# A quantised layer whose weights are rounded earlier, by ScalarE, and whose remainders are made by TensorE

## The chip, the cores and the metric
One core of a Trainium2 chip runs the whole program. The metric is the device time of one execution in microseconds (us). The kernel before takes 1255.05 us (median of 3 runs, 1253.74 to 1255.72). Names used below: PE is TensorE, DVE is VectorE, ACT is ScalarE, POOL is GpSimd, SP is SyncE.

## The reference, cut to what matters
Six layers follow one another on x of shape (4, 16, 16, 192), that is 1,024 tokens of 192 channels: a selective scan, a neighbourhood attention, the quantised layer, a mixture of experts, a full attention, a second mixture of experts. The change concerns the third. In it (12 heads of 16 channels, 4 images of 256 tokens, `fq` rounds to int8 steps of a scale):

```python
x_norm = fq(layernorm(x, g1, beta1), s_n1)          # x is itself a layer-normed t
qkv = fq(einsum(x_norm, fq(w_qkv, s_wqkv)) + b_qkv, s_qkv)
attn = fq(einsum(q, k) * ATTN_SCALE, s_attn)
# integer softmax, on x_int = attn/s - max:
q = floor(x_int / x0_int);  r = x_int - x0_int * q;  z = r + b_int
exp_int = floor((z * z + c_int) * 2 ** (EXP_N - q))
factor = floor(2**32 / sum(exp_int));  out = floor(exp_int * factor / 2**25) / 2**7
x_attn = fq(einsum(einsum(out, v), fq(w_proj)) + b_proj, s_sv);  x = fq(x + x_attn, s_r1)
h = fq(gelu(einsum(fq(layernorm(x)), fq(w_fc1)) + b_fc1));  h = fq(einsum(h, fq(w_fc2)) + b_fc2)
x = fq(x + h, s_r2)
```

## The kernel before, in words
The program is a series of blocks. In a block each engine has its own list of instructions, executed in the order written; semaphores tie the lists together. The layer is `quantised_layer` (line 1014 on).

**Head.** SP loads the scales, seven rows of 192 numbers spread over all partitions, the biases and five weight matrices (lines 1090 and 1092). DVE normalises X into U (lines 165 to 175), makes some 20 constants of one column each (1154 to 1176), scales the seven rows (1179), normalises U into N, multiplies and shifts it by rows and rounds it (1190, 1191, 1140, 1141). Meanwhile POOL rounds the two large weights w1 and w2 (1102 to 1104), and later the projection weight. DVE rounds wqk and wv (1197 to 1199). PE transposes N (1396), makes 12 projections of 128x512 (1408) and 8 of values (1413). ACT evacuates the 12 (1330) and DVE clips and rounds each with two instructions (1140, 1141), then the values. Rounding adds and subtracts the constant MAGIC = 1.5 * 2^23 in float32. POOL copies the operands of four heads at a time to fixed places (1113), and the scores begin (1432).

**Loop.** The function `slots(b, first, second)` of each engine writes the work on images: `first` is the softmax of image b up to its sums, `second` the probabilities and the output of image b-1. The order is image 0 first only, then a loop of three with both, then second only. A slot is one head, and the stages of a head lie in successive slots. With both, an engine's slot n holds, in this order:

- PE: scores of head n into a PSUM bank (1432); four transposes of head n-2's probabilities (1440); four small matmuls of head n-3's output (1449).
- ACT: `shift` of head n+1, which reads the scores and writes lt (1336); two instructions for head n's probabilities pv (1352); the square of head n-1 (1357); the quotient of head n (1362); the copy of head n-1's transposed probabilities (1367).
- DVE: clip of lt (1218), rounding of the quotient of head n-1 (1224), maximum (1227), remainder of head n-1 (1231), the difference x_int of head n (1237), rounding of head n-1's probabilities (1243), and the product and sum for head n-2 (1252).
- POOL: the power of two as an int16 pattern (1121).

The sums of all heads end in a factor on DVE (1258 to 1263), for which ACT waits ahead of the next image.

**After the loop** the output is transposed (1461), projected (1467), requantised, normalised again, and goes through the two feed-forward products (1478, 1486).

**The scan layer** comes first. Its second block has 48 steps. In each, ACT makes one exponential of 128x1020 (line 550) into one of two PSUM pairs, DVE two products and a scan of 128x1024 (465, 472), POOL one product (435), PE the spreads and sums (600, 615). SP prefetches d_sp four steps ahead (419).

Of the kernel before, what the change touches and what calls it, by code (L numbers as in the profile page):

```python
# [14 lines left out]
BF16 = mybir.dt.bfloat16  # L15
# [9 lines left out]
NB = 4  # L25
# [166 lines left out]
KD = 4  # L192
# [6 lines left out]
NSP = 4  # L199


def scan_layer(nc, const, X, D):
# [3 lines left out]
    with ExitStack() as stack:  # L206
# [24 lines left out]
        loaded_g, loaded_w, loaded_p, loaded_s = S("loaded_g"), S("loaded_w"), S("loaded_p"), S("loaded_s")  # L231
        cleared, zeroed, proj, padded, tapped, convd, activated, gated = (
# [43 lines left out]
        with nc.Block() as block:  # L276
            @block.sync
            def _(sp_):
# [107 lines left out]
        ex = ctx.sb("ex", [DI, 2, T])  # L386
# [17 lines left out]
        tile = lambda a, t: a[:, t * P:(t + 1) * P]  # L404
        with nc.Block() as block:
            @block.sync
            def _(sync):
# [18 lines left out]
                for n in range(NSP, N):  # L426
                    spread(n)
# [83 lines left out]
            def _(act):  # L511
# [23 lines left out]
                for i in range(1, KD):  # L535
                    for j in range(2):
                        take(i, j)
                act.wait_ge(A_done, 2)
                for n in range(N):
# [4 lines left out]
                    if n % NG < 2:  # L544
# [462 lines left out]
EXP_N = 30  # L1007
(S_N1, S_WQKV, S_QKV, S_ATTN, S_WPROJ, S_SV, S_R1, S_N2, S_WFC1, S_ACT, S_WFC2, S_M2, S_R2) = range(13)

(K_QKV, K_ATTN, K_X0, K_BI, K_CI, K_INV, K_QB, K_CLAMP, K_NX0, K_PROJ, K_FC1, K_FC2, K_T0, K_T1, K_MAGIC, K_FLOOR) = range(16)  # L1010


def quantised_layer(nc, K, X, D, ln):

    with ExitStack() as stack:
        ctx = Ctx(nc, stack)
        U = ctx.sb("q_U", [P, NT, C])  # L1020
        N = ctx.sb("q_N", [P, NT, C])
        Ni = ctx.sb("q_Ni", [P, NT, C], BF16)
        nT = ctx.sb("q_nT", [CH, 2, T], BF16)
        sc = ctx.sb("q_sc", [P, 13])
        rc = ctx.sb("q_rc", [P, 13])
        kf = ctx.sb("q_kf", [P, 16])
        rows = ctx.sb("q_rows", [P, 7, C])
        bqk = ctx.sb("q_bqk", [P, 6])
        b1 = ctx.sb("q_b1", [P, FT])
        wqk_f = ctx.sb("q_wqk_f", [CH, 2 * 6 * P])  # L1030
        wqk = ctx.sb("q_wqk", [CH, 2 * 6 * P], BF16)
        wv_f = ctx.sb("q_wv_f", [CH, 2 * C])
# [24 lines left out]
        pv = ctx.sb("q_pv", [P, 2, QT, L])  # L1057
        pi = ctx.sb("q_pi", [P, 2, QT, L], BF16)
# [8 lines left out]
        loaded, w_loaded, vec, w_quantised, quantised, first_ln = (  # L1067
            S("loaded"), S("w_loaded"), S("vec"), S("w_quantised"), S("quantised"), S("first_ln"))
        scaled, constants, normed, turned_n, n_sb = S("scaled"), S("constants"), S("normed"), S("turned_n"), S("n_sb")
        proj, evac, qk_ready, v_proj, v_ready = S("proj"), S("evac"), S("qk_ready"), S("v_proj"), S("v_ready")  # L1070
        taken, pool_past = S("taken"), S("pool_past")
        scores, shifted, clipped, negmax, diff, quot, whole, rest, expo, square, expd, factor = (
            S("scores"), S("shifted"), S("clipped"), S("negmax"), S("diff"), S("quot"), S("whole"), S("rest"),
            S("expo"), S("square"), S("expd"), S("factor"))
        prob, floored, turned, turned_sb, summed, o_sb = (
            S("prob"), S("floored"), S("turned"), S("turned_sb"), S("summed"), S("o_sb"))
        o_turned, oT_sb, o_proj = S("o_turned"), S("oT_sb"), S("o_proj")
        act_past = S("act_past")
        h_steps = S("h_steps")
# [4 lines left out]
        SLOTS = NH + 2  # L1084

        with nc.Block() as block:
            @block.sync
            def _(sync):
                for dst, src in ((sc, "q_scales"), (rows, "q_rows"), (bqk, "q_bqk"), (b1, "q_b1")):
                    sync.dma_start(dst[:], D[src].partition_broadcast(P) if src in ("q_scales", "q_rows") else D[src]).then_inc(loaded, 16)  # L1090
                for dst, src in ((wqk_f, "q_wqk"), (wv_f, "q_wv"), (wp_f, "q_wp"), (w1_f, "q_w1"), (w2_f, "q_w2")):
                    sync.dma_start(dst[:], D[src]).then_inc(w_loaded, 16)

            @block.gpsimd
            def _(pool):
                step = Chain(pool, w_quantised)
                pool.wait_ge(scaled, 1)
                pool.wait_ge(w_loaded, 80)

                def quantise(f, i, r):  # L1100
                    n = f.shape[0]
                    step(pool.tensor_scalar(f[:], f[:], rc[0:n, r:r + 1], 127.0, ALU.mult, ALU.min))
                    step(pool.tensor_scalar(f[:], f[:], -128.0, MAGIC, ALU.max, ALU.add))
                    step(pool.tensor_scalar(i[:], f[:], -MAGIC, None, ALU.add))

                quantise(w1_f, w1, S_WFC1)
                quantise(w2_f, w2, S_WFC2)

# [6 lines left out]
                def powers(b, more):  # L1115

                    for h in range(NH):
                        pool.wait_ge(whole, b * NH + h + 1)
# [3 lines left out]
                                           float((127 + EXP_N) * 128), ALU.mult, ALU.add).then_inc(expo, 1)  # L1122
# [13 lines left out]
            def _(v):  # L1136
                step = Chain(v, vec)

                def clip_round(dst, src, signal):
                    step(v.tensor_scalar(src, src, 127.0, -128.0, ALU.min, ALU.max))  # L1140
                    return v.tensor_scalar(dst, src, MAGIC, -MAGIC, ALU.add, ALU.add).then_inc(signal, 1)
# [20 lines left out]
                step(v.tensor_tensor(k(K_QKV), k(K_QKV), r(S_QKV), ALU.mult))  # L1162
                step(v.tensor_scalar(k(K_ATTN), k(K_ATTN), r(S_ATTN), HE ** -0.5, ALU.mult, ALU.mult))
# [9 lines left out]
                step(v.tensor_scalar(k(K_QB), k(K_INV), -0.5, -0.5, ALU.mult, ALU.add))  # L1173
                step(v.tensor_scalar(k(K_CLAMP), k(K_X0), float(EXP_N), None, ALU.mult))
                step(v.tensor_scalar(k(K_NX0), k(K_X0), -1.0, None, ALU.mult))

                step(v.tensor_scalar(bqk[:], bqk[:], r(S_QKV), None, ALU.mult))
                for row, unit in ((0, S_N1), (1, S_N1), (2, S_N2), (3, S_N2), (4, S_QKV), (5, S_SV), (6, S_M2)):
                    step(v.tensor_scalar(rows[:, row, :], rows[:, row, :], r(unit), None, ALU.mult))
                v.memset(kf[:, K_T0:K_T1 + 1], 0.0).then_inc(constants, 1)  # L1180

                def row(i):
                    return rows[:, i, :].unsqueeze(1).broadcast_to([P, NT, C])

                def normed_ints(use, g, beta):

                    v.wait_ge(ln.out, NT * use)
                    ln.vector(v, use, U, N, 1e-6)
                    v.wait_ge(ln.out, NT * (use + 1))
                    step(v.tensor_tensor(N[:], N[:], row(g), ALU.mult))  # L1190
                    step(v.tensor_tensor(N[:], N[:], row(beta), ALU.add))
# [1269 lines left out]
```

## Time and profile before
| | |
|---|---|
| median of the runs shown | 1255.05 us |
| the profiled execution | 1259.88 us, span 1257.9 us |
| busy: PE, DVE, ACT, POOL | 66%, 73%, 48%, 29% of the span |
| granted TensorE clock, mean | 0.795 of full speed |

The profile is of one execution. An interval of idle time is put down to what released the engine. Times of instructions are from their start to the end of their writes, so two instructions of an engine in a row can overlap a little: "spacing" below is from one start to the next. TensorE's clock has two levels, 1.2 GHz (0.50 of full speed) and 2.4 GHz (1.00).

### The profile page before, as it was taken

Reading aid. Unit: us, or ns where it says so; the run is one execution under the profiler, and the core shown is the slowest. Engines: PE = TensorE matmul, PEld = TensorE weight load, DVE = VectorE, ACT = ScalarE, POOL = GpSimd, SP = SyncE. Lnnn points to the kernel's source line nnn. Section 1 sums busy time; section 2 is a strip of 40 time slices with the busy share of each in tenths; the row PEclk is TensorE's granted clock in tenths of the full one; section 3 lists DMA queues with packets and bytes.
Section 4 is the critical chain, followed back from the end, with each engine's and each line's share of the span. In section 5 each row is a group of like instructions: output and inputs, shape, how many; then the busy total and the mean of one; then the engine's idle time right before and its main releaser. Section 6 shows DMA issues by size and latency. Waiting matters only on the chain. (4 is left out here: it accounts for less than half of the span.)

```text
span 1257.9 us, 16849 instructions
## 1 busy us (share of the span) xinstructions
PE 825.4 (66%) x5554; PEld 576.7 (46%) x5554; DVE 921.5 (73%) x1731; ACT 598.2 (48%) x938; POOL 362.2 (29%) x309
## 2 busy tenths in 40 slices
PE   6799999859894041122224336599999747449990
PEld 2333333335783020011114225599888725339990
DVE  5679999936655989999993777488888533628871
ACT  3743333215331046789897223277766122328870
POOL 0036666430000822222210002532222510054444
PEclk8789999969997565555555676899999959659995
DMA  8075565130003000000000008299995110628932
GB/s 258 13 205 151 150 151 150 34 75 1 1 1 88 0 1 1 0 1 0 0 0 1 0 1 224 77 232 267 263 266 160 39 44 1 170 83 258 272 115 81
DMA packets 65821, 120.59 MB, mean 96 GB/s; under 512 B 11152, under 2 KB 40784, under 8 KB 65744
## 3 DMA queue, kind: packets, MB, share of 16 engines
q1 hardware_dynamic: 62672, 113.31, 33.4%
q0 software_dynamic: 3072, 6.30, 1.7%
q8 instruction: 43, 0.70, 0.2%
q14 instruction: 34, 0.28, 0.1%
HBM read 102.08 MB, written 17.50 MB: 95 GB/s over the span
## 5 line engine op out<-in xcount | busy, mean ns | idle before, releaser
L435 POOL TENSOR_TENSOR hC<-hs,Cb 128x1024 f32<-128x1024 f32 x47 | 110.7, 2355 | 129.3 <-DVE hs L472 129.3
L1726 POOL CAST m_h_hi<-m_h 128x512 f16<-128x512 f32 x62 | 54.0, 871 | 247.4 <-DVE m_h L1801 247.4
L472 DVE TENSOR_TENSOR_SCAN hs<-ps_l,dBu 128x1024 f32<-128x1024 f32 x48 | 110.0, 2291 | 2.8 <-ACT ps_l L550 1.2
L1440 PE MATMUL ps_l<-identb,q_pi 128*128 128x128 bf16 x192 | 29.2, 307 | 112.3 <-DVE q_pi L1243 112.3
L550 ACT ACTIVATE ps_l<-d_sp,Am 128x1020 f32<-128x1020 f32 x48 | 53.5, 1115 | 89.9 <-DVE hs L472 89.7
L615 PE MATMUL ps_l<-hC,selT 128*96 128x512 f32 x192 | 93.3, 609 | 1.5 <-POOL hC L435 1.5
L600 PE MATMUL ps_l<-du,sel 96*128 96x512 f32 x192 | 90.5, 593 | 1.4 <-DVE dBu L465 1.4
L1809 DVE TENSOR_TENSOR m_h_lo<-m_h,m_h_hi 128x512 f16<-128x512 f32 x62 | 42.8, 691 | 46.5 <-POOL m_h_hi L1726 41.9
L1121 POOL TENSOR_SCALAR q_e<-q_qi 128x512 int16<-128x512 bf16 x48 | 31.3, 652 | 153.7 <-DVE q_qi L1224 153.7
L1440 PEld LDWEIGHTS ps_l<-identb,q_pi 128*128 128x128 bf16 x192 | 16.5, 130 | 128.4 <-DVE q_pi L1243 128.4
L2092 PE MATMUL ps_m<-m_wd_hi,m_h_hi 128*128 128x192 f16 x248 | 62.9, 254 | 8.4 <-DVE m_h_lo L1809 4.8
L1999 ACT ACTIVATE m_act<-ps_m 128x512 f32<-128x512 f32 x62 | 36.8, 594 | 66.0 <-PE ps_m L2074 55.8
L465 DVE TENSOR_TENSOR dBu<-ps_l,Bb 128x512 f32<-128x512 f32 x96 | 60.7, 673 | 4.9 <-PE ps_l L600 4.8
L2094 PE MATMUL ps_m<-m_wd_hi,m_h_lo 128*128 128x192 f16 x248 | 63.0, 254 | 0.0
L2093 PE MATMUL ps_m<-m_wd_lo,m_h_hi 128*128 128x192 f16 x248 | 63.0, 254 | 0.0
L1432 PE MATMUL ps_l<-q_qkb 16*128 16x256 bf16 x96 | 27.2, 402 | 52.4 <-ACT q_lt L1336 44.4
L1726 POOL CAST g_h_hi<-g_act 128x512 f16<-128x512 f32 x45 | 43.7, 988 | 60.6 <-ACT g_act L2003 60.6
L600 PEld LDWEIGHTS ps_l<-du,sel 96*128 96x128 f32 x192 | 34.2, 188 | 51.2 <-DVE dBu L465 37.2
L615 PEld LDWEIGHTS ps_l<-hC,selT 128*96 128x96 f32 x192 | 27.4, 162 | 58.8 <-POOL hC L435 31.9
L1352 ACT ACTIVATE q_pv<-q_ex,q_kf,q_fac 128x256 f32<-128x256 f32 x96 | 51.8, 591 | 0.5 <-DVE q_fac L1263 0.5
L2070 PE MATMUL ps_m<-m_xt,m_wa_hi 128*128 128x256 f16 x184 | 50.3, 273 | 0.8
L2071 PE MATMUL ps_m<-m_xt,m_wa_hi 128*128 128x256 f16 x184 | 50.2, 273 | 0.0
(484 smaller groups left out, 2807.2 us busy)
## 6 DMA issues: line engine op xcount, KB each, us to landing
d_sp<-scan_d SPq DMA_DIRECT2D x48, 512.0 KB, 4.5
m_sta<-in_m_ua SPq DMA_DIRECT2D x25, 512.0 KB, 4.9
m_stb<-in_m_ub SPq DMA_DIRECT2D x50, 256.0 KB, 6.3
m_std<-in_m_dn SPq DMA_DIRECT2D x25, 384.0 KB, 8.2
g_std<-in_g_dn SPq DMA_DIRECT2D x15, 576.0 KB, 5.9
g_sta<-in_g_ua SPq DMA_DIRECT2D x15, 384.0 KB, 3.5
g_stb<-in_g_ub SPq DMA_DIRECT2D x30, 192.0 KB, 4.7
scratch_x<-zero SPq DMA_DIRECT2D x1, 4416.0 KB, 20.0
```

Of the source, the lines that this page charges most:

```text
L435: pool.tensor_tensor(hC[:, n % 2, :], hs[:, n % 2, :], Cb[:, which(n), :], ALU.mult).then_inc(weighted, 1)
L465: v.tensor_tensor(dBu[:, n % 2, half * BANK:(half + 1) * BANK], ps[:, 4 + half, :], Bb[:, which(n), half * BANK:(half + 1) * BANK], ALU.mu ...
L472: v.tensor_tensor_scan(hs[:, n % 2, ::step], dA(n)[:, ::step], dBu[:, n % 2, ::step], 0.0, ALU.mult, ALU.add).then_inc(scanned, 1)
L550: act.activation(dst[:, :, o:o + L - 1], d_sp[:, n % NSP, :].rearrange("p (b t) -> p b t", t=L)[:, :, o:o + L - 1], ACT.Exp, scale=Am[:, c ...
L600: pe.matmul(ps[:, 4 + half, :], sel[:, n % NG, :], du[:, n // NG, half * BANK:(half + 1) * BANK], start=True, stop=True).then_inc(du_bc, 1)
L615: mm = pe.matmul(ps[0:DI, 6 + half, :], selT[:, n % NG, :], hC[:, n % 2, half * BANK:(half + 1) * BANK], start=(n == STEPS), stop=(m == ST ...
L1352: act.activation(pv[:, h % 2, q, :], ex[:, h, q, :], ACT.Identity, scale=fac[:, h, q:q + 1], bias=kf[:, K_FLOOR:K_FLOOR + 1]).then_inc(pro ...
L1726: pool.tensor_copy(h_hi[:, b % 2, q, :], src).then_inc(h_high, 1)
L2070: pe.matmul(out, wa_hi[a][:, col], x[:, 0, :], start=True, stop=False)
L2092: pe.matmul(out, h_hi[:, b % 2, f // 2, tok], wd_hi[a][:, col], start=(f == 0), stop=False)
L2093: pe.matmul(out, h_hi[:, b % 2, f // 2, tok], wd_lo[a][:, col], start=False, stop=False)
L2094: mm = pe.matmul(out, h_lo[:, b % 2, f // 2, tok], wd_hi[a][:, col], start=False, stop=(f == tiles - 1))
```

## The change
- **Weights.** Scales, inverse scales and the five rounded weight matrices live for the whole program (`K["q"]`). SP loads each float weight into the buffer `ex` of the scan layer, free by then, at scan steps 5, 13, 21, 29 and 37, and ACT rounds it there with four instructions (Identity, Relu, Relu, Identity), one after the exponential of each of four steps. The quantised layer has neither the loads nor the rounding on POOL and DVE.
- **Folded norm.** The two norms ahead of the projections become one: statistics of X once, the second variance worked out from the first, N written once; gain and offset are given in ACT's evacuation of the transposed N as its scale and bias. U is written later, behind image 0. Scaled rows: one ahead of image 0, four behind it.
- **Rounding at ACT's writes.** lt, xi, qi, pi, the operands and the values are fp16 numbers centred at 1536, so that the write itself rounds; DVE's roundings of the quotient (1224) and of the probabilities (1243) are gone, clips stay.
- **Remainders by PE.** Two matmuls of 128x128 by 128x512 fp16 (identity times xi, and -x0 times identity times qi) make the remainder in PSUM bank 5 or 6; ACT squares it in place; DVE's remainder (1231) is gone. DVE takes over the copy of the transposed probabilities, with the centre subtracted.
- **Projections split.** Six projections (images 0 and 1) stand ahead of the loop, six and the values inside the slots of image 0.

The slots after the change, to the order of the instructions:

```diff
 @block.vector, slot n
-  clip lt(h) ; qi = qv + MAGIC - MAGIC (g) ; max(h) ; ri(g) = qi * -x0 + xi ; xi(h) x2
-  pi(g) = pv + MAGIC - MAGIC ; ex(n-2) x2
+  clip lt(h) ; max(h) ; xi(h) x2     # waits rest(h-2)
+  v.wait_ge(turned, pb * NH + g + 1)
+  PT(g) <- ps[2 + g % 2] as F16, - CENTRE
+  ex(n-2) x2                         # from ps[5 + e % 2]
+  if first and not second and 1 <= n < 7: operand(5 + n)
+  if first and not second and 7 <= n < 11: values(n - 7)
 @block.scalar, slot n
   shift(b, h + 1)
-  pv(h) x2 ; square(g) ri -> zz ; quot(h) xi -> qv ; PT(g) <- ps
+  pi(h) x2 (F16) ; square(g) in place in ps[5 + g % 2]   # waits rest(g)
+  quot(h) xi -> qi (F16)
+  if first and not second and n < 6: evacuate(6 + n)
 @block.tensor, slot n
-  h, g, e = n, n - 2, n - 3
+  h, r, g, e = n, n - 1, n - 1, n - 2
   scores(h)
   transposes(g)                      # waits prob(g) instead of floored(g)
+  if first and 0 <= r < NH:
+      pe.wait_ge(quot, b * NH + r + 1)
+      pe.wait_ge(expd, (b * NH + max(r - 1, 0)) * QT)
+      pe.matmul(ps[:, 5 + r % 2, :], K["identh"], xi[:, r % 2], start=True, stop=False)
+      pe.matmul(ps[:, 5 + r % 2, :], XI[:, :], qi[:, r % 2, :], start=False, stop=True).then_inc(rest, 1)
   output(e)
+  if first and not second and n < 6: project(6 + n)
+  if first and not second and 6 <= n < 10: project_values(n - 6)
```

In the scan layer:

```diff
 @block.sync
   for n in range(NSP, N):
+      w = (n - Q_FIRST) // Q_EACH        # Q_FIRST = 5, Q_EACH = 8
+      if (n - Q_FIRST) % Q_EACH == 0 and w < len(q_weights):
+          sync.wait_ge(soft_vec, 3 * KD) if w == 0 else sync.wait_ge(qw["quantised"], 4 * w)
+          sync.dma_start(staged(w)[:, :], D[q_weights[w][0]]).then_inc(q_loaded, 16)
       spread(n)
 @block.scalar
   exponential of step n
+      w, i = divmod(n - Q_FIRST, Q_EACH)
+      if w >= 0 and i < 4 and w < len(q_weights):
+          integer(w, i)    # i = 0 waits q_loaded; then Identity, Relu, Relu, Identity
```

## Rows read from the trace of the kernel before

**Rows 1.** Busy time by engine in two stretches, the layer's head and its loop:
```profile
396.00:466.00 70.00, 12.37 (x60) 6.31 (x60) 63.50 (x129) 12.45 (x17) 31.76 (x14) 0.56 0.14 40
...
514.00:560.00 46.00, 13.04 (x104) 7.69 (x104) 44.44 (x122) 42.55 (x70) 9.09 (x15) 0.50 0.00 1
```
**Rows 2.** Instructions in order of time, head; start, duration, engine, line:
```profile
396.86 2.18 DVE L165 BATCH_NORM_STATS2 ln_st<-X 128x6 f32<-128x192 f32 x8 [2.40 <-PEq L56]
...
398.16 0.43 SPq L1090 DMA_DIRECT2D q_b<-in_q_b  x1
...
403.16 0.93 DVE L1161 TENSOR_TENSOR q_kf<-q_sc 128x1 f32<-128x1 f32 x5
...
408.46 24.23 DVE L1179 TENSOR_SCALAR q_rows<-q_rows,q_rc 128x192 f32<-128x192 f32 x7
...
432.66 3.14 POOL L1104 TENSOR_SCALAR q_w<-q_w_f 128x1152 bf16<-128x1152 f32 x1
...
448.39 8.57 PE L1408 MATMUL ps_l<-q_nT,q_wqk 96*128 96x512 bf16 x24 [2.08 <-DVE q_wv L1199]
...
460.43 2.11 POOL L1113 COPY q_qkb<-q_qk 128x256 bf16<-128x256 bf16 x6 [24.64 <-DVE q_qk L1141]
...
465.46 0.61 PE L1432 MATMUL ps_l<-q_qkb 16*128 16x256 bf16 x4 [7.18 <-DVE q_vi L1141]
```
**Rows 3.** In order of time, loop with both stages, one head:
```profile
546.96 0.41 DVE L1243 TENSOR_SCALAR q_pi<-q_pv 128x512 bf16<-128x512 f32 x1
...
547.42 0.60 PE L1440 MATMUL ps_l<-identb,q_pi 128*128 128x128 bf16 x4 [2.81 <-DVE q_pi L1243]
...
547.82 0.30 PE L1449 MATMUL ps_l<-q_vi,q_PT 128*128 x4
...
548.05 0.60 PE L1432 MATMUL ps_l<-q_qkb 16*128 16x256 bf16 x2
...
548.69 0.78 ACT L1336 ACTIVATE q_lt<-ps_l,q_kf 128x512 f32<-128x512 f32 x1
...
549.37 0.91 DVE L1231 SCALAR_TENSOR_TENSOR q_ri<-q_qi,q_kf,q_xi 128x512 bf16<-128x512 bf16 x1
549.37 1.08 ACT L1352 ACTIVATE q_pv<-q_ex,q_kf,q_fac 128x256 f32<-128x256 f32 x2
...
550.35 0.71 ACT L1357 ACTIVATE q_zz<-q_ri,q_kf 128x512 f32<-128x512 bf16 x1
550.85 0.41 DVE L1243 TENSOR_SCALAR q_pi<-q_pv 128x512 bf16<-128x512 f32 x1
550.97 0.81 ACT L1362 ACTIVATE q_qv<-q_xi,q_kf 128x512 f32<-128x512 bf16 x1
```
**Rows 4.** Issues of transfers at the layer's start; KB each, us from issue to landing:
```profile
q_b<-in_q_b SPq DMA_DIRECT2D x1, 3.0 KB, 3.5
```
**Rows 5.** DVE's groups by shape, whole span; busy, mean ns of one, idle before:
```profile
L1224 DVE TENSOR_SCALAR q_qi<-q_qv 128x512 bf16<-128x512 f32 x48 | 19.9, 415 | 3.4 <-ACT q_qv L1362 3.4
...
L741 DVE CAST n_Q<-ps_l 96x512 f16<-96x512 f32 x12 | 8.2, 682 | 1.1 <-PE ps_l L890 1.1
...
L1141 DVE TENSOR_SCALAR q_Ni<-q_N 128x1536 bf16<-128x1536 f32 x2 | 1.9, 960 | 0.1
...
L1780 DVE COPY m_xd<-ps_m 128x768 f16<-128x768 f16 x2 | 1.1, 558 | 1.2 <-PE ps_m L2021 1.2
```
**Rows 6.** In order of time, first instruction of each image, of the drain, and behind it:
```profile
513.93 1.45 ACT L1336 ACTIVATE q_lt<-ps_l,q_kf 128x512 f32<-128x512 f32 x2 [3.08 <-DVE q_fac L1263]
...
565.22 1.45 ACT L1336 ACTIVATE q_lt<-ps_l,q_kf 128x512 f32<-128x512 f32 x2 [0.97 <-DVE q_fac L1263]
...
666.53 2.07 ACT L1352 ACTIVATE q_pv<-q_ex,q_kf,q_fac 128x256 f32<-128x256 f32 x4 [0.54 <-DVE q_fac L1263]
...
686.27 3.65 PE L1461 MATMUL ps_l<-ident,q_Os 128*96 128x128 f32 x16 [0.67 <-ACT q_Os L1372]
```
**Rows 7.** In order of time, one step of the scan layer on ACT:
```profile
82.32 1.11 ACT L550 ACTIVATE ps_l<-d_sp,Am 128x1020 f32<-128x1020 f32 x1 [2.39 <-DVE hs L472]
```

More of the change, by code:

```diff
@@ L199 @@
 NSP = 4
+Q_FIRST = 5
+Q_EACH = 8
 def scan_layer(nc, const, X, D):
@@ L298, in _ @@
                 pool.memset(const["all"][:, :], 1.0).then_inc(constants, 1)
+                for n, value in enumerate((MAGIC, 128.0 - MAGIC, 255.0, 127.0)):
+                    pool.memset(qw["steps"][:, n:n + 1], value).then_inc(constants, 1)
             @block.vector
@@ L1084, in quantised_layer @@
         SLOTS = NH + 2
+        LATE = (2, 3, 4, 7)
+        order = [(half, o) for half in range(NHALF) for o in range(6)]
+        home = lambda n: n % 4 if n < 6 else LATE[n % 4]
         with nc.Block() as block:
@@ L1088, in _ @@
             def _(sync):
[L1089 to L1092, printed above, removed]
+                for dst, src in ((cols, "q_cols"), (rows, "q_rows"), (bqk, "q_bqk"), (b1, "q_b1")):
+                    sync.dma_start(dst[:], D[src].partition_broadcast(P) if src == "q_rows" else D[src]).then_inc(loaded, 16)
             @block.gpsimd
             def _(pool):
[L1096 to L1107, printed above, removed]
                 def take(b, group):
@@ L1162, in _, with integers @@
                 step(v.tensor_tensor(k(K_QKV), k(K_QKV), r(S_QKV), ALU.mult))
+                v.tensor_scalar(bqk[:], bqk[:], r(S_QKV), CENTRE, ALU.mult, ALU.add).then_inc(scaled, 1)
+                def integers(dst, part, src, steps, at, signal):
+                    v.tensor_scalar(part, src, -CENTRE, 127.0, ALU.add, ALU.min).then_inc(steps, 1)
+                    v.wait_ge(steps, at)
+                    v.tensor_scalar(dst, part, -128.0, None, ALU.max).then_inc(signal, 1)
+                for n in range(2 * NHALF):
+                    half, c = divmod(n, 2)
+                    at = slice(half * BANK, (half + 1) * BANK)
+                    v.wait_ge(centred, n + 1)
+                    integers(nT[:, c, at], nh[:, c, at], nh[:, c, at], n_part, n + 1, n_ready)
                 step(v.tensor_scalar(k(K_ATTN), k(K_ATTN), r(S_ATTN), HE ** -0.5, ALU.mult, ALU.mult))
@@ L1172, in _ @@
                 step(v.reciprocal(k(K_INV), k(K_X0)))
-                step(v.tensor_scalar(k(K_QB), k(K_INV), -0.5, -0.5, ALU.mult, ALU.add))
+                step(v.tensor_scalar(k(K_QB), k(K_INV), -0.5, CENTRE - 0.5, ALU.mult, ALU.add))
                 step(v.tensor_scalar(k(K_CLAMP), k(K_X0), float(EXP_N), None, ALU.mult))
[L1175 to L1191, printed above, removed]
-                    clip_round(Ni[:], N[:], normed)
@@ L1201, in _, with operand @@
+                step(v.tensor_scalar(k(K_SQUARE), k(K_XC), CENTRE, k(K_BI), ALU.mult, ALU.add))
+                v.tensor_scalar(XI[:, :], K["ident"][:, :], k(K_XC), -1.0, ALU.mult, ALU.mult).then_inc(constants, 1)
+                def operand(n):
+                    half, o = order[n]
                     v.wait_ge(evac, n + 1)
-                    clip_round(qk[:, n * BANK:(n + 1) * BANK], qf[:, n % 4, :], qk_ready)
-                for n in range(NT // 2):
+                    at = o * T + half * BANK
+                    integers(qk[:, at:at + BANK], qh[:, n % 4, :], qh[:, n % 4, :], q_part, n + 1, qk_ready)
@@ L1211, in slots @@
+                for n in range(6):
+                    operand(n)
                 def slots(b, first, second):
@@ L1271, in _, with clip_round, row @@
                 v.wait_ge(factor, NB)
+                def clip_round(dst, src, signal):
+                    step(v.tensor_scalar(src, src, 127.0, -128.0, ALU.min, ALU.max))
+                    return v.tensor_scalar(dst, src, MAGIC, -MAGIC, ALU.add, ALU.add).then_inc(signal, 1)
+                def row(i):
+                    return rows[:, i, :].unsqueeze(1).broadcast_to([P, NT, C])
                 def requantised(src, unit, add_to, out_unit):
@@ L1421, in slots @@
+                for n in range(6):
+                    project(n)
+                pe.wait_ge(constants, 1)
                 def slots(b, first, second):
@@ L1451, in slots @@
                             mm.then_inc(summed, 1)
+                        if first and not second and n < 6:
+                            project(6 + n)
+                        if first and not second and 6 <= n < 10:
+                            project_values(n - 6)
                 slots(0, True, False)
+                pe.wait_ge(v_ready, 4)
                 with pe.Fori(1, NB) as b:
```

341 lines of the change are left out of this document (195 added, 146 removed).

## The prediction
> **What bounds the kernel now.** I read two windows first. In the layer's head DVE is busy 63.5 of 70 us while PE is busy 12.4; in the loop DVE is busy 44.4 of 46 us, ACT 42.6 counted with overlaps, PE 13.0, and the granted clock is 0.50, the lower level, throughout [rows 1]. So DVE sets both. Then the timeline. The head runs from the first statistics at 396.86 to the first scores at 465.46, 68.6 us. The reader is to see one odd row: seven scalings of a 192-column row take 24.23 us, 3.46 each, and they end when POOL comes to the last of its roundings of w1 and w2 (432.66) [rows 2]. In the loop one DVE instruction comes back every 3.89 us (546.96 to 550.85): that is the price of a head, DVE's instructions back to back [rows 3]. An image is 51.3 us (513.93 to 565.22), the first 48.5 (465.43 to 513.93), three with both stages 152.6 (513.93 to 666.53), the drain 19.7 (to 686.27) [rows 2, 6].
>
> **The head.** Gone are POOL's rounding and with it the 24 us, the second statistics, gain, offset, rounding of N and of wqk, wv on DVE, and six of twelve projections plus the values. I count what is left from 396.86 as time 0.
> Statistics of X (2.2) and 0.7 more, as now. The column operations wait for the last of four loads: issued at 398.16 and 3.5 to land, so 4.8 [rows 2, 4]. Two column operations, four of the second variance, a square root on ACT and back, two more: nine small instructions of 0.19 (five in 0.93 [rows 2]) and two handovers, to 6.9. Eight writes of N at 0.30 each (five such stretches of 192 columns by the 0.53 ns a column below, plus overhead) end at 9.3. PE transposes them as it arrives, 16 at 0.23 (3.65 for 16 [rows 6]), to 10.9; ACT's four evacuations of 0.78 with 0.68 spacing [rows 3] end near 12.2. DVE has nine more constants (10.9), then two clips for each of four pieces.
> A clip of fp16 into fp16 or bf16 is not in this trace. From above: the same with a float32 side, 0.415 for 512 columns; with 0.960 for 1,536 that is 0.53 ns a column and 0.14 fixed [rows 5]. From below: the fixed part. Nearest on 16-bit data: out of PSUM, float32 512 columns cost 0.682, fp16 768 columns 0.558, so a column costs half [rows 5]. I halve the column here too: 0.28 for 512, spacing 0.20; a clip pair is 0.52 (0.79 by the upper row).
> Two pieces are done at 12.0, all at 13.0. 21 constants at 0.19 follow on DVE, to 17.1; PE's first projections (0.86 for two matmuls at the lower clock) and ACT's first four evacuations lie beside them. Six operands at 0.52: 20.2. POOL's first two copies, 0.35 each (2.11 for six [rows 2]): scores at 21.0. I add 0.5 for gaps: 21.5, and -47.1 us. With the upper price it is 24.2.
> The Trainium skill (VectorE: DVE Perf Modes, "What auto-detection actually checks") lets a one-source instruction with 16-bit data on both sides in SBUF take four elements a cycle where float32 takes two; that is the halved column, and the trace has no row for it. Were the page wrong, its absence would cost the 2.7 us named.
>
> **The loop: sums.** A head on DVE loses the rounding of the quotient, that of the probabilities and the remainder (0.34 + 0.34 + 0.83 in spacing) and gains the copy of PT (0.34), which ACT loses: from 3.89 to about 2.5 [rows 3, 5]. ACT has `shift` 0.68, two pi 0.98, square 0.58 to 0.62, quotient 0.81: 3.05 [rows 3]. By sums a head would be ACT's 3.0. PE gains two matmuls of 512 columns, 0.43 each (24 took 8.57, part at the upper clock; 0.43 is 512 columns at 1.2 GHz) [rows 2].
>
> **The loop: order.** The sum is not what ends last. PE's list says: scores(n+1), transposes(n), rest(n), output(n-1), then scores(n+2). rest(n) waits for quot(n), which is the last instruction of ACT's slot n; and ACT's slot n+1 begins with shift(n+2), which waits for scores(n+2). In between ACT can do nothing, its list is in order: pi(n+1), square(n) and quot(n+1) stand behind shift(n+2). So one head is a ring:
> - shift to quotient's end on ACT: 0.68 + 0.98 + 0.58 + 0.81 = 3.05 (548.69, 549.37, 550.35, 550.97 and its 0.81; the copy of PT that sits between two heads is gone) [rows 3];
> - handover 0.05 (547.37 to 547.42), two rest matmuls 0.86, output 0.23 (547.82 to 548.05), scores 0.60, handover 0.04 (548.65 to 548.69): 1.80 [rows 3].
> Together 4.85 us a head against 3.89. DVE and POOL lie inside it: clip, maximum and difference need 2 us after a shift and have nearly a whole head.
> Before, the same place held a softer ring: transposes, output, scores, 1.27 us, with ACT's copy of PT beside them [rows 3].
> What the fp16 clips cost does not matter here: DVE has 2 us to spare in either case.
>
> An image with both stages, from its first shift: shift(2) at 5.0 (quotient of head 0 at 2.5 to 3.3, rest, scores), shift(11) nine rings later at 48.6, quot(10) to 51.7, square(10) behind rest(10), quot(11) to 54.2, rest 1.1, square 0.7, DVE's two products 0.95, factor and handover 1.6: 58.6. Three: 175.7 against 152.6, +23.1.
>
> Image 0: no pi (0.98 less) but a projection of 0.86 behind rest in PE slots 0 to 5 and two tiles of values (0.64) in 6 to 9. ACT's part of a ring is 2.07, PE's 2.41, then 2.19, then 1.55. shift(2) is at 6.3, four rings of 4.48, four of 4.26, one of 3.62: shift(11) at 44.9; the same end: 53.8. ACT's evacuations and DVE's operands fit inside. Then DVE writes four scaled rows and U (12 instructions, about 4.6) ahead of its first clip, of which 3.6 are late for the next image. 57.4 against 48.5: +8.9.
>
> **The drain** has on ACT only pi, 12 x 0.98, and 2.3 behind it (transposes, copy, output, Os): 14.0 against 19.7, -5.7 [rows 3, 6].
>
> **Scan layer.** A rounding of 1,536 columns is below 1.5 x 1.11 = 1.67, against 2.39 that ACT idles in a step [rows 7]; 20 of them, hidden, 0. A load is issued some four steps ahead of its use, a step being 3.5. If the cover were gone: up to 20 x 1.6.
>
> **Sum.** -47.1 + 8.9 + 23.1 - 5.7 = -20.8. Behind the loop nothing changes. The profiled run was 1259.88 and the median is 1255.05; the change is taken off both alike: 1234.3 as a median.
>
> **Rivals.**
> 1. *The clock rises in the loop.* PE would be busy about half of a head (0.61 for transposes, 1.71 in one run) where it is busy 28% now at 0.50; the head's 12 us of work did lift the mean there to 0.56 [rows 1]. At 2.4 GHz rest, output and scores take about 1.0, a ring 4.1: 0.74 less for 30 rings and 1.1 less for ten, -33 if always, -17 if half the time: 1218. Against it: each rise shortens PE's share and so undoes itself. The Trainium skill (TensorE: Matmul & The Clock Gate, "Part 1: The HAM clock gate") says that the default is throttled and activity releases it, which speaks for this case; it names no case such as scores on 16 rows. Chance 0.2.
> 2. *ACT's sum sets the pace*, PE running ahead of the ring: 3.05 a head. 1.80 less for 30 rings and 1.8 less for ten: 1234 - 72 = 1162. It needs scores(n+2) not to stand behind rest(n), and in the order of the diff they do. Chance 0.07.
> 3. *Slower: the roundings in the scan steps are not hidden.* If a step with one grows by its whole 1.6 and the first of each matrix waits for its load too (five waits of 2), +42: 1276. It decides from +21 us on, about 1.0 for each of the 20 steps. For it: the steps' scan on DVE waits on ACT's exponential; against it: the 2.39 idle in each step. Chance 0.08.
> 4. *The stall of 24 us has another cause than POOL's roundings* and stays with the scaled rows: five rows instead of seven, +17, and 1251. Against it: the same instruction's first cases in the row and its end with POOL's work. Chance 0.03.
>
> **Chances.** The forecast holds 0.62, its own range 1222 to 1247 from the head's clip prices (3), gaps in the ring (0.2 for 40 rings, 8) and some rise of the clock in image 0 (-5). Faster by over 0.2% (2.5 us, about what a measurement of this kernel can tell): 0.88; within 0.2%: 0.03; slower 0.09. The range takes in half of rival 1: 1208 to 1249.
>
> **What would show it.** First scores 21 to 24 us after the layer's first statistics. In the loop ACT's `shift` idle about 1.8 us, released by PE's scores, and PE's rest matmuls released by ACT's quotient; a head 4.8 to 4.9 us; DVE busy near 55%; clock 0.50. Image 0 near 57 us, the others near 58.6, the drain near 14. Scan steps still 3.5 us. Heads of 3.0 to 4.2 us or a scan step over 3.6 would make it wrong.

## The result and the profile after

The changed kernel takes 1239.38 us (median of 4 runs, 1238.26 to 1242.96) beside 1254.67 us for the kernel before on the same chip (4 runs, 1253.74 to 1255.72): ratio 0.9883, 95% interval 0.986 to 0.9905, that is 15.3 us less, where 20.8 less was forecast. The profiled execution of the changed kernel took 1238.26 us, its span is 1236.5 us.

The head first, in order of time (start, duration, engine, line; in brackets the idle time ahead and what ended it). It answers to [rows 2]:
```profile
391.45 2.18 DVE L1169 BATCH_NORM_STATS2 q_st<-X 128x6 f32<-128x192 f32 x8 [2.49 <-PEq L56]
...
396.12 0.22 DVE L1176 TENSOR_SCALAR q_cols<-q_cols,q_rc 96x2 f32<-96x2 f32 x1 [1.75 <-DMA q_b<-in_q_b]
...
398.03 2.41 DVE L1187 TENSOR_SCALAR q_N<-X,q_mv,q_rs 128x192 f32<-128x192 f32 x8
...
403.21 2.88 PE L1457 MATMUL ps_l<-q_nT,q_wqk 96*128 96x512 bf16 x12 [1.34 <-DVE q_nT L1201]
...
408.33 0.29 DVE L1199 TENSOR_SCALAR q_qh<-q_qh 128x512 f16<-128x512 f16 x1
...
411.79 2.11 POOL L1132 COPY q_qkb<-q_qk 128x256 bf16<-128x256 bf16 x6 [144.22 <-DVE q_qk L1201]
...
412.67 0.58 PE L1486 MATMUL ps_l<-q_qkb 16*128 16x256 bf16 x2 [6.58 <-POOL q_qkb L1132]
```
From the first statistics to the first scores it is 21.2 us, where it was 68.6: the row of 24.23 us is gone, and so are the second statistics and the roundings.

One head of the loop with both stages, in order of time, beside [rows 3]:
```profile
484.43 0.61 PE L1500 MATMUL ps_l<-q_xi,identh 128*128 128x512 f16 x1 [0.75 <-ACT q_qi L1407]
...
484.83 0.63 PE L1501 MATMUL ps_l<-q_qi,q_XI 128*128 128x512 f16 x1
...
485.25 0.30 PE L1508 MATMUL ps_l<-q_vi,q_PT 128*128 x4
...
485.49 0.60 PE L1486 MATMUL ps_l<-q_qkb 16*128 16x256 bf16 x2
486.13 0.78 ACT L1381 ACTIVATE q_lt<-ps_l,q_kf 128x512 f16<-128x512 f32 x1 [1.83 <-PE ps_l L1486]
486.81 1.08 ACT L1397 ACTIVATE q_pi<-q_ex,q_kf,q_fac 128x256 f16<-128x256 f32 x2
486.94 0.29 DVE L1253 TENSOR_SCALAR q_lt<-q_lt 128x512 f16<-128x512 f16 x1 [1.99 <-ACT q_lt L1381]
...
487.79 0.64 ACT L1401 ACTIVATE ps_l<-ps_l,q_kf 128x512 f32<-128x512 f32 x1
...
488.36 0.81 ACT L1407 ACTIVATE q_qi<-q_xi,q_kf 128x512 f16<-128x512 f16 x1
...
489.30 0.60 PE L1500 MATMUL ps_l<-q_xi,identh 128*128 128x512 f16 x1 [0.75 <-ACT q_qi L1407]
```
Read it as a ring: TensorE's remainder waits for ScalarE's quotient, output and scores stand behind the remainder, ScalarE's `shift` waits 1.83 us for the scores, and the next quotient stands behind `shift`. The remainder comes back after 4.87 us (484.43 to 489.30), where a head cost 3.89 before. VectorE, which had hardly a gap before, is idle 1.99 us ahead of its clip.

The first instruction of each image, and of the drain, on ScalarE, and the first behind the drain on TensorE (beside [rows 6]):
```profile
467.59 1.45 ACT L1381 ACTIVATE q_lt<-ps_l,q_kf 128x512 f16<-128x512 f32 x2 [2.54 <-DVE q_fac L1288]
...
473.92 0.81 ACT L1407 ACTIVATE q_qi<-q_xi,q_kf 128x512 f16<-128x512 f16 x1 [3.91 <-DVE q_xi L1260]
...
530.31 1.45 ACT L1381 ACTIVATE q_lt<-ps_l,q_kf 128x512 f16<-128x512 f32 x2 [2.22 <-DVE q_fac L1288]
...
589.20 1.45 ACT L1381 ACTIVATE q_lt<-ps_l,q_kf 128x512 f16<-128x512 f32 x2 [2.22 <-DVE q_fac L1288]
...
647.93 11.90 ACT L1397 ACTIVATE q_pi<-q_ex,q_kf,q_fac 128x256 f16<-128x256 f32 x24 [2.06 <-DVE q_fac L1288]
...
661.96 3.65 PE L1525 MATMUL ps_l<-ident,q_Os 128*96 128x128 f32 x16 [0.67 <-ACT q_Os L1414]
```
Image 0 takes 54.9 us from the first scores, the three images 62.7, 58.9 and 58.7, the drain 14.0. The 62.7 holds a wait of 3.91 us for VectorE, which writes the scaled rows and U first.

Busy time by engine in the head and in image 1 (columns as in [rows 1]):
```profile
391.00:413.00 22.00, 6.61 (x30) 4.12 (x30) 16.74 (x84) 8.81 (x13) 1.21 (x4) 0.66 0.08 23
...
468.00:530.00 62.00, 26.54 (x144) 11.01 (x144) 38.62 (x124) 36.62 (x61) 9.49 (x18) 0.50 0.00 1
```
In the loop no engine is near full: VectorE 62%, ScalarE 59%, TensorE 43%, at a granted clock of 0.50. With no engine near full and one short wait coming back in every head, a ring is the thing to suspect; the experiments test it.

The scan layer, by groups (busy us, mean ns of one, idle ahead):
```profile
L587 ACT ACTIVATE ps_l<-d_sp,Am 128x1020 f32<-128x1020 f32 x48 | 53.5, 1115 | 71.5 <-DVE hs L495 71.3
...
L571 ACT ACTIVATE ex<-ex,q_steps,q_rc 96x1536 f32<-96x1536 f32 x2 | 3.3, 1652 | 0.0
```
ScalarE's idle time ahead of the exponentials has shrunk from 89.9 to 71.5 us, and the 48 steps take 164.7 us as before (76.49 to 241.2, and 72.41 to 237.1): the 20 roundings went into idle time. Those of 1,536 columns, the longest, took 1.56 us, or 1.65 with a scale as in the row.

### The profile page after: what moved, and what is told of

Its sections match the earlier page's. It is cut to its first block and busy times, and to the rows that moved or that the text cites. A ratio compares the mean times of both kernels' runs of the same rounds, so it can differ in the third digit from the quotient of the medians.

```text
span 1236.5 us, 16872 instructions
## 1 busy us (share of the span) xinstructions
PE 868.6 (70%) x5650; PEld 585.1 (47%) x5650; DVE 830.0 (67%) x1627; ACT 590.7 (48%) x912; POOL 327.1 (26%) x304
## 5 line engine op out<-in xcount | busy, mean ns | idle before, releaser
L587 ACT ACTIVATE ps_l<-d_sp,Am 128x1020 f32<-128x1020 f32 x48 | 53.5, 1115 | 71.5 <-DVE hs L495 71.3
L1494 PE MATMUL ps_l<-identh,q_pi 128*128 128x128 f16 x192 | 29.1, 307 | 78.1 <-ACT q_pi L1397 78.1
L1140 POOL TENSOR_SCALAR q_e<-q_qi 128x512 int16<-128x512 f16 x48 | 30.4, 632 | 193.9 <-ACT q_qi L1407 118.4
L1381 ACT ACTIVATE q_lt<-ps_l,q_kf 128x512 f16<-128x512 f32 x48 | 37.1, 778 | 84.4 <-PE ps_l L1486 74.5
L1500 PE MATMUL ps_l<-q_xi,identh 128*128 128x512 f16 x48 | 29.1, 606 | 55.2 <-ACT q_qi L1407 55.2
L2067 ACT ACTIVATE m_act<-ps_m 128x512 f32<-128x512 f32 x62 | 36.8, 594 | 62.2 <-PE ps_m L2142 58.1
L1253 DVE TENSOR_SCALAR q_lt<-q_lt 128x512 f16<-128x512 f16 x48 | 14.1, 293 | 73.7 <-ACT q_lt L1381 73.4
L1494 PEld LDWEIGHTS ps_l<-identh,q_pi 128*128 128x128 f16 x192 | 16.5, 130 | 95.1 <-ACT q_pi L1397 95.1
L1397 ACT ACTIVATE q_pi<-q_ex,q_kf,q_fac 128x256 f16<-128x256 f32 x96 | 50.8, 589 | 2.1 <-DVE q_fac L1288 2.1
```

Of the source, the lines that this page charges most:

```text
L587: act.activation(dst[:, :, o:o + L - 1], d_sp[:, n % NSP, :].rearrange("p (b t) -> p b t", t=L)[:, :, o:o + L - 1], ACT.Exp, scale=Am[:, c ...
L1397: act.activation(pi[:, h % 2, q, :], ex[:, h, q, :], ACT.Identity, scale=fac[:, h, q:q + 1], bias=kf[:, K_FLOOR:K_FLOOR + 1]).then_inc(pro ...
L1494: mm = pe.transpose(ps[:, 2 + g % 2, 0:L].bitcast(F16)[:, kt * L + q * P:kt * L + (q + 1) * P], pi[:, g % 2, q, kt * P:(kt + 1) * P], K["i ...
```

## The experiments

Theory: the loop is bound by the ring of one quotient, one remainder, one scores, one `shift`, because TensorE's list puts the next scores behind a remainder that waits for ScalarE's last instruction. Main rival: the new work has its price in any order.

**Scores one head ahead.** The changed kernel, but for one thing:
```diff
-                        if first and h < NH:
+                        for h in ((0, 1) if n == 0 else (n + 1,)):
+                            if not first or h >= NH: continue
                             ... scores(h)
```


> The changed kernel, with PE's scores one head earlier in its list: scores(n+1), transposes(n-1), rest(n-1), output(n-2). Ring theory (quotient on ACT, rest, output and scores on PE, then shift on ACT, 4.87 us a head in the profile after): the ring is cut, ACT's own sum of 3.05 us a head is next, DVE's 2.8 just under it; 30 heads with both stages and 10 of image 0 lose 1.5 to 1.8 each, so 1239 - 64 = 1175 us (1165 to 1190), and ACT's wait for scores ahead of its shift goes from 1.83 to under 0.2 us. Rival A (the loop is slow because PE at the lower clock is short of time, or because each fp16 write or PSUM read is slower than counted, not because of the order): within 10 us of 1239. Rival B (DVE's chain of clip, maximum and difference inside one slot is next at once): a head of 3.8 to 4.0 us, about 1205.

Measured: 1168.23 us (1167.93 to 1171.44), ratio 0.929 (0.9257 to 0.9324). In order of time, one head:
```profile
474.00 0.82 ACT L1407 ACTIVATE q_qi<-q_xi,q_kf 128x512 f16<-128x512 f16 x1
...
474.71 0.78 ACT L1381 ACTIVATE q_lt<-ps_l,q_kf 128x512 f16<-128x512 f32 x1
...
474.95 0.60 PE L1502 MATMUL ps_l<-q_xi,identh 128*128 128x512 f16 x1 [0.72 <-ACT q_qi L1407]
...
475.37 1.10 ACT L1397 ACTIVATE q_pi<-q_ex,q_kf,q_fac 128x256 f16<-128x256 f32 x2
...
476.35 0.65 ACT L1401 ACTIVATE ps_l<-ps_l,q_kf 128x512 f32<-128x512 f32 x1
...
476.92 0.82 ACT L1407 ACTIVATE q_qi<-q_xi,q_kf 128x512 f16<-128x512 f16 x1
```
and the loop's busy time:
```profile
460.00:590.00 130.00, 82.80 (x486) 37.22 (x485) 110.01 (x357) 115.17 (x200) 26.71 (x48) 0.50 0.00 1
```
Inside an image no wait stands ahead of `shift` any more, ScalarE runs almost without a gap, and a head is its sum, 2.92 us. The same instructions in another order are 71 us faster by the medians (69.4 from the layer's start to the end of the drain in the profiles, 74 by the ratios): the theory holds. The clock is 0.50 although TensorE is busy for 64% of the time.

**A third matmul in the remainder**, in the order of the change:
```diff
-  pe.matmul(ps[5 + r % 2], identh, xi, start=True, stop=False)
+  pe.matmul(ps[5 + r % 2], identh, xi, start=True, stop=True)
+  pe.matmul(ps[5 + r % 2], identh, xi, start=True, stop=False)
```


> The changed kernel with one matmul more per head in the rest group (identity times xi written once more ahead of the two, its result overwritten), 0.43 us at the lower clock. Ring theory: every head of the 40 or so in the ring grows by the whole 0.43, +17 to +19 us over the changed kernel, 1257; a head 5.30 us. Rival A (PE has slack, since it is busy 43% of the loop): 0, 1239. Rival C (the added work lifts the clock in the loop): below 1239, heads near 4.2.

Measured: 1259.73 us (1257.24 to 1263.79), ratio 1.0014 (0.9998 to 1.003). Over the changed kernel that is 20 us by the medians and 16 by the ratios. ScalarE's `shift`, twice in a row:
```profile
501.04 0.78 ACT L1381 ACTIVATE q_lt<-ps_l,q_kf 128x512 f16<-128x512 f32 x1 [2.26 <-PE ps_l L1486]
...
506.33 0.78 ACT L1381 ACTIVATE q_lt<-ps_l,q_kf 128x512 f16<-128x512 f32 x1 [2.26 <-PE ps_l L1486]
```
A head is 5.29, 0.42 more, and the wait for scores grows by as much (1.83 to 2.26). In the profiles each of the four images is 5.1 us longer, 20.5 together: all 48 heads pay, where 40 were expected to. TensorE is far from busy and yet each of these microseconds counts: they lie on the ring.

**The same third matmul, with the scores ahead** (both diffs together).


> Scores one head ahead, and the same third matmul of 512 columns in each head's rest group that cost 17 to 20 us in the order of the change. Theory (the ring over ScalarE and TensorE was the price; with the ring cut TensorE is no longer in series with ScalarE, and has about 0.4 us of slack ahead of the square): 0 to +4 us against the kernel with the scores ahead, 1168 to 1172. Rival (the remainders on TensorE cost their own time in any order): +17 us, about 1185.

Measured: 1173.88 us (1171.42 to 1179.11), ratio 0.9341 (0.931 to 0.9372), 5.6 us over the kernel with the scores ahead, by medians of different runs. The square now waits:
```profile
496.96 0.66 ACT L1401 ACTIVATE ps_l<-ps_l,q_kf 128x512 f32<-128x512 f32 x1 [0.65 <-PE ps_l L1504]
```
In the profiles it is 4.2 us up to the end of the drain. That is a fifth to a third of the price in the ring, and a little more than the 0 to 4 expected: TensorE's slack ahead of the square was 0.37 us (475.98, the end of the second matmul, to 476.35), less than the matmul's 0.43. A head is 3.01 where it was 2.92. Each of the three images is 1.7 us longer than with the scores ahead alone (41.3 against 39.6 for the second), about half of it where one image ends and the next begins; image 0 is not longer.

**The remainder back on VectorE**, all else as changed: VectorE makes it as float32 with one scalar_tensor_tensor, ScalarE squares it from there into PSUM, TensorE's two matmuls are gone.
```diff
+  v.scalar_tensor_tensor(ri[g % 2], qi[g % 2], k(K_T0), xi[g % 2], MULT, ADD)   # K_T0 = -x0
-  pe.matmul(... identh, xi ...) ; pe.matmul(... XI, qi ...)
-  act.activation(ps[5 + g % 2], ps[5 + g % 2], Square)
+  act.activation(ps[5 + g % 2], ri[g % 2], Square)
```


> The changed kernel with the remainder given back to DVE (one scalar_tensor_tensor of 128x512, as before, between the maximum and the difference); the two rest matmuls are gone and ACT squares from SBUF into PSUM. All else of the change stays. Ring theory: PE's part of the ring is gone; DVE's sum becomes 3.3 to 3.4 us a head, ACT's 3.1: heads of 3.4 to 3.6, about 1.35 less in 30 and about 1.0 less in 10 of image 0: 1239 - 50 = 1189 us. Rival A (the remainders on PE were a relief of DVE and the loop is slow for another reason): slower than 1239, since DVE gets 0.83 us a head more: up to +40.

Measured: 1186.1 us (1183.86 to 1188.14), ratio 0.9418 (0.9384 to 0.9452). In order of time:
```profile
485.76 0.78 ACT L1389 ACTIVATE q_lt<-ps_l,q_kf 128x512 f16<-128x512 f32 x1 [0.44 <-PE ps_l L1495]
486.31 0.74 DVE L1262 SCALAR_TENSOR_TENSOR q_ri<-q_qi,q_kf,q_xi 128x512 f32<-128x512 f16 x1
...
489.00 0.78 ACT L1389 ACTIVATE q_lt<-ps_l,q_kf 128x512 f16<-128x512 f32 x1 [0.17 <-PE ps_l L1495]
```
A head is 3.0 to 3.5 us, VectorE almost without a gap. So in the order of the change the part "remainders by PE" costs 53 us by the medians (58 by the ratios) of what the rest of the change had won: it takes 0.8 us from VectorE's sum, but its two matmuls, 0.9 us, tie ScalarE's quotient to the next scores, and that closes the ring.

**The quotient on VectorE**, in the order of the change:
```diff
+  v.tensor_scalar(qi[h % 2], xi[h % 2], k(K_INV), k(K_QB), MULT, ADD)   # behind xi(h)
-  act.activation(qi[h % 2], xi[h % 2], Identity, scale=K_INV, bias=K_QB)
```


> The order of the change, the quotient of each head written by VectorE (tensor_scalar, 512 half-precision elements, about 0.3 us) in place of ScalarE's 0.81 us. Theory: the ring stays, scores - shift - ... - rest - scores, but is shorter by about 0.5 us where the quotient was on it, 4.87 to 4.3 a head: 48 x 0.5 = -24, about 1215 us (1205 to 1225). Rival (the ring runs over ScalarE's list alone, so that taking 0.81 from it frees all of that, and VectorE's 3.2 us a head are not waited for): 4.05 a head, -39, about 1200.

Measured: 1207.42 us (1206.26 to 1208.11), ratio 0.96 (0.9584 to 0.9616). In order of time:
```profile
497.45 0.78 ACT L1385 ACTIVATE q_lt<-ps_l,q_kf 128x512 f16<-128x512 f32 x1 [1.72 <-PE ps_l L1484]
498.13 1.08 ACT L1401 ACTIVATE q_pi<-q_ex,q_kf,q_fac 128x256 f16<-128x256 f32 x2
...
499.27 0.61 PE L1492 MATMUL ps_l<-identh,q_pi 128*128 128x128 f16 x4 [1.93 <-ACT q_pi L1401]
...
499.67 0.63 PE L1498 MATMUL ps_l<-q_xi,identh 128*128 128x512 f16 x1
...
500.75 0.60 PE L1484 MATMUL ps_l<-q_qkb 16*128 16x256 bf16 x2
...
501.47 0.78 ACT L1385 ACTIVATE q_lt<-ps_l,q_kf 128x512 f16<-128x512 f32 x1 [1.72 <-PE ps_l L1484]
```
The ring is still there (`shift` waits 1.72 us for the scores), but runs another way: behind the probabilities instead of the quotient, `shift`, two pi, transposes, remainder, output, scores, 4.02 us. Quotient and square both left it and the transposes, 0.40, came in; the 4.3 expected had taken out 0.5 only. The 1207 lie in the range of the theory, 8 us below its middle. The rival's number for a head was near (4.05) for a reason that the wait contradicts.

**The weights alone**: the kernel before with nothing but the scan layer's roundings and without those on POOL and VectorE. The edit on the kernel before:
```diff
 @block.scalar, scan steps
+  integer(w, i)                           # 20 instructions, as in the change
 @block.gpsimd, quantised_layer
-  quantise(w1_f, w1) ; quantise(w2_f, w2) ; quantise(wp_f, wp_f)
 @block.vector, quantised_layer
-  rounding of wqk, wv ; reciprocal of the scales
```


> The kernel before with one part of the change only: scales and the five weight matrices rounded by ACT in the scan steps; POOL's and DVE's roundings and loads in the quantised layer are gone, all else as before. Theory: the seven scaled rows cost 0.32 us each instead of 3.46 (-22.0), DVE's roundings of wqk and wv go (-4.1), the scan steps stay at 3.50 us: 1254.7 - 26 = 1228.5 us. Rival (the stall of 24 us has another cause than POOL's roundings): rows stay at 3.46, only -4: 1250. Rival (roundings in the scan steps are not hidden): steps 13 to 44 grow and part of the 26 is given back, up to 20 x 1.6: 1228 to 1260.

Measured: 1236.47 us (1234.41 to 1239.7), ratio 0.9833 (0.9797 to 0.9869): 20.6 us less. In order of time:
```profile
402.64 2.45 DVE L1191 TENSOR_SCALAR q_rows<-q_rows,q_rc 128x192 f32<-128x192 f32 x7
...
436.48 0.61 PE L1439 MATMUL ps_l<-q_qkb 16*128 16x256 bf16 x4 [7.12 <-DVE q_vi L1155]
```
The same seven scaled rows take 2.45 us where they took 24.23 [rows 2], with no rounding on POOL beside them; the head is 45.2 us (from 391.32), 23.4 less. The scan steps are as long as before (161.2 us from the second exponential to the last), so the roundings are hidden here too. The 26 us expected were too many. VectorE's roundings of wqk and wv had stood in time in which it would have waited for the projections: without them it waits 5.18 us ahead of its first clip, where it waited 1.94. The loop is 1.0 longer, and this profile has the longer of the two tails told of below.

From the layer's start to the end of the drain, in the profiles, this part alone wins 22.5 us (289.4 to 267.0) and all five together 18.9 (to 270.5). The medians, 20.6 and 15.3, point the same way, but the intervals of the ratios overlap a little.

**The kernel before, scores ahead**, the first diff on it.


> The kernel before, with TensorE issuing each head's scores one head earlier and nothing else changed. Theory (before, VectorE's instructions stood back to back at 3.89 us a head and TensorE's place in the order cost nothing; the ring was made by the change, which put the remainders between quotient and scores): 0 us, 1253 to 1259. Rival (the order of the scores held back the kernel before as well, so that the gain of the scores ahead has little to do with the change): 0.3 us or more a head, 1243 or less.

Measured: 1256.18 us beside 1258.33, ratio 0.9983 (0.9966 to 1.0). VectorE's rounding of the probabilities, twice:
```profile
546.50 0.41 DVE L1243 TENSOR_SCALAR q_pi<-q_pv 128x512 bf16<-128x512 f32 x1
...
550.40 0.41 DVE L1243 TENSOR_SCALAR q_pi<-q_pv 128x512 bf16<-128x512 f32 x1
```
3.90 us a head, as before, and 289.4 us from the layer's start to the end of the drain in both profiles. Where VectorE had hardly a gap the order on TensorE was worth nothing; the interval of the ratio leaves room for 4 us at most. The change made the ring the bound.

**Scores ahead, U and four rows late.**
```diff
-  scaled rows 0, 1, 3, 4 and U(0..7)     # ahead of image 1
   loop of images, drain
+  scaled rows 0, 1, 3, 4 and U(0..7)     # behind VectorE's last head
```


> Scores one head ahead, and VectorE's four scaled rows and eight U tiles, which stood between the second half of the first head group and the first clamp of image 1, moved behind the last head. Theory (in the kernel with the scores ahead ScalarE's own sum paces the loop; its one long wait, 3.9 us for q_xi at the start of image 1, is VectorE's 3.29 us of U and some 0.5 us of rows): the wait goes, the work lands beside the drain, where VectorE has little else; 1168 - 3.6 = about 1164.5 us (1162 to 1167). Rival (VectorE, with about 2.8 us a head, is as much the pace as ScalarE, or U is waited for behind the drain): no gain, 1167 to 1171.

Measured: 1164.52 us (1162.72 to 1171.26), ratio 0.9274 (0.924 to 0.9308). Image 1 is 39.7 us where it was 43.5 with the scores ahead alone (458.89 to 502.37), 3.8 less; the medians, of different runs, differ by 3.7.

**With the quotient on GpSimd besides:**
```diff
+  pool.tensor_scalar(qi[h % 2], xi[h % 2], kf[K_INV], kf[K_QB], MULT, ADD)
-  act.activation(qi[h % 2], xi[h % 2], Identity, scale=K_INV, bias=K_QB)
```


> Scores ahead and U late, and the quotient of each head written by GpSimd (tensor_scalar, 512 half-precision elements, one scalar pointer for each of its two steps) in place of ScalarE's 0.81 us. ScalarE's sum falls from 2.92 to 2.1 us a head, VectorE's of about 2.75 becomes the pace. Theory A (GpSimd's instructions of this size leave VectorE's alone): 2.75 to 2.8 a head, 48 x 0.15 = -7, about 1157 us (1152 to 1163). Theory B (VectorE's clips, differences and copies stretch while GpSimd works, as its scaled rows did beside the roundings of w1 and w2, 3.46 against 0.3 us): slower than 1164.5, 1170 us or more, with VectorE's instruction of 0.29 us at 0.5 or more where it lies beside GpSimd's.

Measured: 1160.42 us (1158.03 to 1163.54), ratio 0.9222 (0.9194 to 0.9249), the fastest median; its interval and the one above still overlap. From the layer's start to the end of the drain the profiles say 6.5 us less. The time is that of theory A; what theory B says of VectorE's instructions is seen too, in image 0. In order of time:
```profile
426.20 0.73 POOL L1146 TENSOR_SCALAR q_e<-q_qi 128x512 int16<-128x512 f16 x1 [0.22 <-POOL q_qi L1141]
426.37 0.71 DVE L1259 TENSOR_SCALAR q_lt<-q_lt 128x512 f16<-128x512 f16 x1
...
506.58 0.29 DVE L1259 TENSOR_SCALAR q_lt<-q_lt 128x512 f16<-128x512 f16 x1
...
506.85 0.62 POOL L1146 TENSOR_SCALAR q_e<-q_qi 128x512 int16<-128x512 f16 x1 [0.32 <-DVE q_ex L1279]
```
The last two rows are of image 2. There GpSimd's instructions fall beside VectorE's products and maximum, the clip takes 0.29, and the image takes 36.8 us (496.10 to 532.85) instead of 39.7. In image 0 the clip meets GpSimd: five of its twelve clips take 0.71, where two did with the quotient on ScalarE, and the image takes 45.7 (414.05 to 459.71) instead of 43.1. That the clips are all of these 2.5 us is not shown.

**The changed kernel once more.**


> The changed kernel once more beside the others: 1238 to 1243 us, head period 4.87 us in the last three images; the tail behind the drain, from the last ScalarE read of the scores to the next layer, again about 69.5 us if the lower granted clock of the projections belongs to the kernel, 66.9 if it was chance.

Measured: 1242.09 us (1239.01 to 1244.38) beside 1257.8, ratio 0.9885 (0.9868 to 0.9902). The projections behind the drain, first in the profile of the result, then in this one, by window:
```profile
660.00:672.00 12.00, 10.22 (x48) 9.47 (x48) 1.41 (x3) 2.87 (x5) 0.00 (x0) 0.54 0.01 1
```
```profile
662.00:674.00 12.00, 9.52 (x59) 8.59 (x56) 2.87 (x5) 2.87 (x5) 0.00 (x0) 0.80 0.00 1
```
One kernel shows both: a granted clock of 0.54, 32 projections that are busy for 7.8 us, and 69.5 us from the drain to the next layer; or 0.80, 5.5 and 66.9. Of the twelve profiles of this case five have the longer tail (69.2 to 69.7) and seven the shorter (66.8 to 67.2).

## Why the prediction was right, and where it was off

- **What bounds the kernel now:** right, as far as it was tried. In the loop VectorE had hardly a gap, and moving the scores in TensorE's list did nothing. No run shortened VectorE's list in the loop and left the rest as it was.
- **The head, -47.1:** right, 68.6 to 21.2, -47.4. The fp16 clip, priced by halving the column, was 0.28 and took 0.28 to 0.29. The stall was POOL's roundings (weights alone: 2.45 for 24.23); rival 4 falls. The 3.46 us for each scaled row is a mean of two kinds: two rows took 0.32 before POOL began, and five 4.1 to 5.4.
- **The order in the loop, 4.85 a head:** right, 4.87. The wait of `shift` is 1.83 where 1.8 was named. VectorE is busy 62%, not "near 55%"; the terms given for its head (3.89 less 1.51, plus 0.34) add up to 2.7 and not to "about 2.5". Nothing in the forecast rests on that.
- **An image with both stages, 58.6:** 58.7 to 58.9; with 3.9 us of the first taken off, three are 176.4 against 175.7.
- **Image 0, 53.8 and 3.6 late:** 54.9 and 3.9. The ring there is 4.57 against 4.48 while operands are projected, mostly because two projections hold TensorE 0.99 us (422.18 to 423.17), not 0.86; after them it is 4.36 against 4.26.
- **The drain, 14.0:** 14.0. **The scan steps, 0:** 164.7 both times; rival 3 falls (a rounding of 1,536 columns took 1.56 to 1.65, below the bound of 1.67).
- **Rival 1, the clock rises:** no, 0.50 throughout the loop, and even at the 64% of the loop with the scores ahead. The Trainium skill's account (TensorE: Matmul & The Clock Gate, "Part 1: The HAM clock gate") that activity releases the throttled clock was cited for this rival; this loop does not show it, though behind the drain the clock did rise (0.54 and 0.80 above).
- **Rival 2, ScalarE's sum sets the pace:** not in the order of the diff; in the other order exactly that, 2.92 where 3.05 was written.

The step that was off is "Behind the loop nothing changes": in the profile shown it is 69.5 us where it was 66.9, and that is TensorE's clock, which is not of the change, since the same kernel has both. In the profile up to the end of the drain the change is -18.9 (289.4 to 270.5) against -20.8 forecast, the missing 1.9 being image 0 and the images; with the tail it is -16.3, and the medians say -15.3, with an interval of about 2.8 on either side.

The tail does not settle that difference. In the repeat it is the shorter one, the change up to the end of the drain is -19.1, and the medians still say -15.7. Of these 3.4 us the cause stays open. Executions differ in stretches that the change does not touch: from the start of the next layer to the end, the same code takes 503.5 to 507.0 us in the twelve profiles. Nor is the change of span, 21.4, a proof of the forecast: in the profiled execution of before the layer began at 396.86, in all eleven others at 391.3 to 394.9, and the shorter way there (here 5.4) is no work of this change. What decides TensorE's clock behind the drain in an execution stays open too.

So a change that takes 47 us from the head and 6 from the drain gives 34 back in the loop, by the place of one group of matmuls in TensorE's list. Written with the scores ahead it is worth 89 us (ratio 0.929).

## What to carry to other kernels

When work moves from a full engine to an idle one, don't compare sums: write each engine's list for one period, draw every wait between them, and look for a closed path; its length is the pace, however idle the engines are. A producer whose inputs have long been ready (here the scores) belongs ahead of any instruction that waits for the same consumer. And measure the parts alone: one may be worth more than the whole.

## What the runs showed of the hardware

Some of VectorE's instructions between SBUF tensors wait for GpSimd's. The seven scaled rows of the kernel before, one by one: two took 0.32 us, and then five in a row each lasted until 0.11 to 0.12 us after the end of one of GpSimd's roundings. One such pair:
```profile
414.55 5.39 POOL L1103 TENSOR_SCALAR q_w_f<-q_w_f 96x1536 f32<-96x1536 f32 x1
414.61 5.44 DVE L1179 TENSOR_SCALAR q_rows<-q_rows,q_rc 128x192 f32<-128x192 f32 x1
```
Without the roundings all seven took 2.45 us. The clip of 0.29 took 0.71 when it began 0.17 us behind GpSimd's, and ended 0.15 us after that one's end (427.08 and 426.93), as if it had waited for the whole of it. The Trainium skill (SBUF — State Buffer, "SBUF: two separate sides") says that GpSimd and VectorE, the latter in some kinds of instruction only, share one pair of ports, which the first to start keeps for its whole instruction; these rows agree.

Not every pair is like that. VectorE's products, which read PSUM, were not stretched beside GpSimd's quotient (0.48 us); those of the kernel before, which read SBUF, took 0.60 to 0.83 in the seven cases beside GpSimd and 0.47 alone. And one clip was stretched, but ended before GpSimd's instruction did:
```profile
462.64 1.74 POOL L1102 TENSOR_SCALAR q_wp_f<-q_wp_f,q_rc 96x384 f32<-96x384 f32 x1
462.78 1.25 DVE L1140 TENSOR_SCALAR q_vf<-q_vf 128x1536 f32<-128x1536 f32 x1
```
The same clip took 0.96 with the weights alone, where nothing ran beside it. A wait for GpSimd's whole instruction does not explain this one.
